# Unread products in TensorE's queue at the end of attention and ahead of the expert blocks of a decoder layer

## The reference

```
x = layernorm(x + self_attention(x))        # 16 heads of 64, rotary on half of each head, causal
x = layernorm(x + cross_attention(x, ctx))  # 16 query heads of 8, 4 key/value heads, two masks
x = layernorm(x + experts(x))               # experts(x) = x + the two best of 8 experts, weighted

gates  = sinkhorn((x @ router_w.T + router_b) / max(temperature, 0.1), 3 iterations)
top 2  -> weights normalised to a sum of 1
expert = (relu(x @ wg) * (x @ wp)) @ wo     # 128 -> 256 -> 128
```

## Time and profile before

| | us |
|---|---|
| runs | 963.95, 965.68, 969.04 |
| median | 965.68 |
| the profiled execution | 965.04 |
| its span | 963.2 |

### The profile page before, as it was taken

How to read it: one execution, slowest core, us unless ns; L and a number is a source line. 1 busy time by engine, 2 the same in 40 slices (tenths; PEclk the granted TensorE clock), 3 DMA queues, 4 the chain that set the end, 5 groups by cost and what they waited for, 6 DMA issues and landing times. The chain is left out here.

```text
span 963.2 us, 23090 instructions
## 1 busy us (share of the span) xinstructions
PE 822.4 (85%) x7560; PEld 655.1 (68%) x7592; DVE 721.1 (75%) x1995; ACT 684.0 (71%) x2437; POOL 657.4 (68%) x714
## 2 busy tenths in 40 slices
PE   3579999999999999899998899978888669899990
PEld 2467777777777777677777777767666347677760
DVE  4658888888888877888889888879965336755674
ACT  3368888888888887888888788857778325454564
POOL 4487766777777777777777677755678714577771
PEclk7799999999999999999999999989999659999995
DMA  4000317900000000000000000000001151114434
GB/s 130 6 7 13 120 33 133 94 19 15 13 8 12 7 16 7 13 7 12 14 10 12 7 13 7 16 4 7 7 26 42 48 141 35 34 55 138 141 102 131
DMA packets 63507, 39.81 MB, mean 41 GB/s; under 512 B 15936, under 2 KB 60224, under 8 KB 63392
## 3 DMA queue, kind: packets, MB, share of 16 engines
q1 hardware_dynamic: 58848, 28.89, 13.8%
q0 software_dynamic: 4544, 9.45, 2.9%
HBM read 21.51 MB, written 16.81 MB: 40 GB/s over the span
## 5 line engine op out<-in xcount | busy, mean ns | idle before, releaser
L407 POOL TENSOR_TENSOR crossed<-raw,sinT 128x512 f32<-128x512 f32 x128 | 162.8, 1282 | 147.4 <-ACT raw L528 141.5
L513 ACT ACTIVATE prob<-ps,negmax 128x128 f32<-128x128 f32 x512 | 181.3, 386 | 72.1 <-DVE negmax L690 72.1
L521 ACT ACTIVATE xprob<-ps,xmax 128x128 f32<-128x128 f32 x512 | 136.1, 415 | 2.8
L401 POOL TENSOR_TENSOR prob<-prob,recip 128x512 f32<-128x512 f32 x128 | 132.0, 1043 | 4.2 <-DVE recip L695 4.0
L1761 POOL DMA_INDIRECT answered<-ysb,goes_to x78 | 76.8, 984 | 58.3 <-DVE ysb L1852 42.8
L513 ACT ACTIVATION_READ_ACCUMULATOR prob<-ps,negmax 128x1 f32 x512 | 115.6, 226 | 0.0
L690 DVE TENSOR_REDUCE negmax<-ps 128x4 f32<-128x512 f32 x128 | 84.0, 678 | 31.5 <-PE ps L990 31.5
L924 PE MATMUL ps<-ident,xprob 128*128 128x128 f32 x514 | 82.3, 284 | 15.3 <-DVE xprobT L652 6.5
L528 ACT ACTIVATE raw<-ps 128x512 f32<-128x512 f32 x128 | 80.1, 626 | 15.7 <-POOL crossed L407 10.3
L962 PE MATMUL ps<-xT_hi,w_lo 128*128 128x256 f32 x256 | 81.7, 319 | 7.2 <-DVE qR L702 6.1
L416 POOL TENSOR_TENSOR kR<-kR,crossed 128x512 f32<-128x512 f32 x60 | 76.7, 1278 | 14.0 <-DVE kR L702 12.9
(11 more groups left out here) (224 smaller groups left out, 2259.5 us busy)
## 6 DMA issues: line engine op xcount, KB each, us to landing
xg<-placed SPq DMA_DIRECT2D x8, 528.0 KB, 5.8
yq<-answered SPq DMA_DIRECT2D x8, 512.0 KB, 5.6
placed<-fw_hi SPq DMA_DIRECT2D x1, 3008.0 KB, 18.6
xf<-in_x SPq DMA_DIRECT2D x32, 64.0 KB, 2.7
xres<-in_x SPq DMA_DIRECT2D x32, 64.0 KB, 1.9
cx<-in_ctx SPq DMA_DIRECT2D x32, 64.0 KB, 1.8
out_y<-yo SPq DMA_DIRECT2D x8, 256.0 KB, 2.4
placed<-fw_hi SPq DMA_DIRECT2D x1, 1984.0 KB, 25.7
```

The lines of the kernel that those rows point to most:

```text
L401: nc.gpsimd.tensor_tensor(prob[:, n], prob[:, n], recip[:, n, :, None].broadcast_to([128, 4, S]), ALU.mult).then_inc(normed, 1)
L407: nc.gpsimd.tensor_tensor(crossed[n % 2][:], raw[n % 2][:, ::-1], sinT[:, :, None, :].broadcast_to([128, 2, 2, S]), ALU.mult).then_inc(sin ...
L513: last = nc.scalar.activation(prob[:, n, j, :], bank(name)[:, j * S:(j + 1) * S], ACT.Exp, bias=negmax[:, n, j:j + 1], accum_out=sums[:, n ...
L521: last = nc.scalar.activation(xprob[:, n, g, :], bank(name)[:, g * S:(g + 1) * S], ACT.Exp, bias=xmax[:, n, g:g + 1])
```

## The change

A function `busy(s, n)` puts n products of `identb` and `causal` (128x512, bf16) into bank 7, in slots 34 and 35 only. Nothing reads them, they wait for nothing, and no semaphore counts them. In slot 34 there are 27 of them, in slot 35 there are 22, each group right behind the step that is named ahead of it. Eight more follow the last slot, ahead of the end of attention's block. In the experts' part, three fp32 products of the identity with itself (128x128) go into bank 4 behind `x_transpose(0)`; `expert_down(0)` overwrites them later. Nothing else changes.

```
+                def busy(s, n):
+
+                    if s < B + 2:
+                        return
+                    for _ in range(n):
+                        nc.tensor.matmul(ps[:, 7, :], identb[:], causal[:].rearrange("p j s -> p (j s)"), start=True, stop=True)
...
                         xprob_transpose(0)
+                        busy(s, 2)
...
                         xprob_transpose(1)
+                        busy(s, 2)
                         xprob_transpose(2)
+                        busy(s, 2)
...
                         xprob_transpose(3)
+                        busy(s, 3)
                         xpv()
+                        busy(s, 2)
                     if on(a):
                         xc_transpose()
+                        busy(s, 1)
                     if on(c):
                         xo_back()
+                        busy(s, 2)
                     if on(a):
                         xqkv()
+                        busy(s, 1)
...
                         xo_transpose()
+                        busy(s, 1)
...
                         xout()
+                        busy(s, 6)
...
                         xqk_transpose()
+                        busy(s, 3)
...
                         x2_transpose()
+                        busy(s, 2)
...
             slots(pe, slot)
+            for _ in range(8):
+                nc.tensor.matmul(ps[:, 7, :], identb[:], causal[:].rearrange("p j s -> p (j s)"), start=True, stop=True)
...
                     if i == 0:
                         x_transpose(0)
+                        for _ in range(3):
+                            nc.tensor.matmul(ps[:, DOWN, 0:128], ident[:], ident[:], start=True, stop=True)
```

## The result

The kernel before takes 965.9 us (median of 8 runs, 963.95 to 969.04), the changed one 960.0 us (8 runs, 956.42 to 962.08). The ratio over all runs is 0.9932, with a 95% interval from 0.9915 to 0.9949: faster by 0.7%. The two medians lie 5.9 us apart, 0.6%. The forecast of 964.2 was wrong by 4.2 us, and its range (961.0 to 967.5) lies above the time. It came out as rival A had it, in number (960.7) and in mechanism.

A forecast was written before the change was run, and what follows sets the result against it. TensorE's half clock, over some 41 us around attention's end, was taken as the only place to win. Barrier -0.93, three products +0.25 and first blocks -0.8 sum to -1.5 us: 965.7 to 964.2 us, range 961.0 to 967.5.

The forecast's parts named there:

- rival A: Attention's barrier: POOL's drain follows the layernorm, not the last scatter; about -5.0 us, giving 960.7 us; chance 0.13.
- The clock stays up in the slots: Slots 34 and 35: fillers make TensorE 0.90 busy, so its clock should stay at 1.00 until they end.
- rival B: Clock falls in slot 34 and the tail's fillers hold the barrier: 969.4 us, half form 966.7; chance 0.12 together.
- The price of a filler, 0.215 us: Each added unread product on TensorE costs 0.215 us at full clock and about 0.43 at half.
- Slot 34: POOL's 0.93 us wait ahead of xr goes, and no more; each later scatter starts 0.93 us earlier.
- Slot 35: Full clock saves 3.2 us together on cross attention's chain in its last batch, 2.7 of it ahead of mv.
- The barrier: End of attention: POOL's drain ends 9.8 us after the last scatter's start, so the barrier gains only 0.93 us.
- The clock falls over the barrier: TensorE does nothing for 3.8 us from last filler to first transpose, so its clock is down when the blocks begin.
- The three products of ident: Ahead of x_transpose(1): at half clock they cost 0.25 us beyond their wait, but help the clock rise near 786.
- The first blocks, 0.8 us, with 2.0 as the upper end: Experts' first four blocks: an earlier clock rise wins 0.8 us, 0 if it stays down, 2.0 at most.
- The shift goes through to the end: Second group's routing, scatters and final joins start by block index, so the shift reaches the end in full: -1.5 us.
- C: Nothing moves: clock up in attention, but xt no earlier and the blocks cold; +0.25 us, 965.9 us; chance 0.13.

The follow-up runs named there:

- e4: Changed kernel with each filler in bank 7 replaced by two fp32 transposes of the identity: 960.84 us, 0.9941 of the kernel before.
- e6: Changed kernel without the fillers in slots 34 and 35, the eight and the three products kept: 964.76 us, 0.999 of the kernel before.
- e7: Changed kernel without the eight products, with the last batch's rstd on ScalarE instead of POOL: 959.53 us, 0.9928 of the kernel before.
- e5: Kernel before with 20 more scatters, to scratch nobody reads, ahead of the 40: 994.81 us in one profiled run (before 966.6).
- e1: Changed kernel with only the fillers of slots 34 and 35, without the eight and the three: 962.85 us, 0.996 of the kernel before.
- e2: Changed kernel without the eight products ahead of the barrier: 961.17 us, 0.9951 of the kernel before.
- e3: Changed kernel without the three products behind x_transpose(0): 960.66 us, 0.9942 of the kernel before.
- e14: The changed kernel again, unaltered, where the kernel before takes about 1014 us: 1011.44 us, 0.9971 of the kernel before.
- e10: The changed kernel once more, unaltered, where the kernel before took 1014.39 us: 1016.96 us, 1.0017 of the kernel before.

## Why the prediction was wrong, by its own steps

1. **The clock stays up in the slots**: right; 1.00 in every stretch from 744.5 to 792.4. The rule on transposes by which rival B would have been likelier (the Trainium skill, TensorE: Matmul & The Clock Gate, Part 4: PE-mode transpose) did not show itself in e4.
2. **The price of a filler, 0.215 us**: right; six take 1.46 us and eight 1.89. Where the clock is low it is 0.43 (e6). In the slots they are not quite free: in slot 34 xqkv starts 0.90 us behind xo_back in after and 0.88 in before, since two fillers take what the full clock gives there. xr waits for nothing even so.
3. **Slot 34**: right; xr's wait of 0.93 us is gone and the last scatter comes 0.84 us earlier, counted from slot 34 (27.05 us in before, 26.21 in after).
4. **Slot 35**: right in kind. The two savings ahead of mv were to bring rstd 0.93 + 2.7 = 3.6 us forward; it starts 4.2 earlier (32.65 us behind the start of slot 34, then 28.49). The 2.7 are exact, counted from the first xprob transposes of slot 35. The 0.93 was too small: these transposes come 1.5 us earlier (18.33 us behind the start of slot 34, then 16.87), since the steps of slot 34 behind xr (xqk_transpose, xscores) run at full clock too. Their rows, in before and in after:

```profile
762.78 2.15 PE L924 MATMUL ps<-ident,xprob 128*128 128x128 f32 x8 [0.38 <-ACT xprob L521]
```

```profile
762.38 0.66 PE L924 MATMUL ps<-ident,xprob 128*128 128x128 f32 x4 [0.62 <-ACT xprob L521]
```

5. **The barrier**: wrong, and this is the step that failed. "I take it that the drain ends 9.8 us after the last scatter has started, whatever the layernorm does." It does not. With 40 scatters it ends 3.35 us behind POOL's last calculation (before, after), or behind the last scatter where no calculation follows (e7), and with 60 scatters 5.0 us behind (e5): 0.082 us for each scatter in the block. So the barrier moved with rstd: 4.2 us without the eight (e1, e2), 3.9 with them, not 0.93. In the profiles this is 3.0 us of the error, and the blocks, which won 2.2 us where the sum has 0.55 (0.8 less 0.25), are 1.7 more, which follows from it. The medians moved by 5.9 us where the sum had 1.5.
6. **The clock falls over the barrier**: wrong as a consequence. With the barrier 3 us earlier than forecast TensorE idles 1.3 us and not 3.8, and the clock stays. In e2, where the idle time is 2.8 us, it falls and comes back as the prediction described.
7. **The three products of ident**: the 0.25 us at half clock do not arise at full clock; there they are of no use (e3). Without the eight they win 1.5 us (e1, e2).
8. **The first blocks, 0.8 us, with 2.0 as the upper end**: 2.2, a little above that end, since all six blocks run at full clock.
9. **The shift goes through to the end**: right up to block 46, to 0.03 us. At block 47 the executions of after and e1 lost 1.8 and 1.5 us by the load and the fall of the clock behind it; of the nine profiles of the table only these two have it.

The rivals: A was right in its mechanism and nearly in its size (-3.4 and -1.3 to -2.0, measured -3.9 and -2.2), and in that the eight are then last at the barrier: TensorE's drain is, by 0.25 us, and e1 and e2 show that they cost 0.27. B's price exists (e6), but not the low clock that it needs. C did not happen. The forecast had given A 0.13. Of the signs that it named, the one for B ("if TensorE's drain is the last") turned out to fit A too; the one for A, POOL's drain within 3.5 us of rstd, came true. What misled the forecast was to weigh "9.8 us found twice" above the plain row, which showed POOL's drain ending 3.4 us behind rstd. Two sums of unlike terms that agree were no evidence: in the earlier trace rows 6.4 us lie between the scatter's start and the end of POOL's work, at the program's end the scatter is itself the last work.

## What to carry to other kernels

Unread products in TensorE's waits are a cheap way to hold its clock over a thin stretch, if each group is shorter than the wait that it lies in (here 0.215 us for each) and if the clock is up when they run; at half clock the same ones cost twice (0.43 us) and can become the last to finish at a barrier (e6). When you ask what a barrier waits for, count POOL's drain from the end of POOL's own last instruction, and give it a price for each indirect DMA that it has issued in the block. And count savings from one event inside the execution: profiled executions of kernels that are alike up to the change differ by up to 4.4 us ahead of it (742.6 to 747.0).

## What the runs showed of the hardware

- POOL's drain behind indirect DMAs cost 0.082 us for each of them, in the block that ends, with about 65 KB in each: 3.35 us with 40, 5.0 with 60 and 8.4 with 102. It is paid whole behind the last instruction, even where that ends 2.1 us (after) or 5.5 us (before) after the last scatter has left POOL. The start that the profile gives for the drain can lie well ahead of it (764.3 in e7, six scatters early).
- fp32 transposes held TensorE at 2.4 GHz like products: 1.00 from 744.5 to 778.8 us with transposes as the fillers (e4).
- An idle time of 1.31 us at the barrier with fillers ahead of it left the clock up (after), one of 1.54 us without them did not (e7), nor did 2.81 (e2). These runs also differ in what TensorE did on both sides of it, so the length of the idle time alone is not shown to decide.
- The same program, changed or not, took 966 us in some runs and 1014 in others. In the latter TensorE, VectorE and ScalarE idle for microseconds while POOL goes on with its scatters, and a gain of 0.6% did not repeat (0.9971 in e14, 1.0017 in e10).
